# A prologue in another order: mask split and written earlier, cond turned later, presets and mask rows moved

## The reference

```python
xn = layer_norm(x, norm_w, norm_b)
q = (xn @ q_w + q_b).reshape(Bx, Tx, H, -1)
k = (xn @ k_w + k_b).reshape(Bx, Tx, H, -1)
att = jnp.einsum('bnhl,bmhl->bnmh', q, k)
att = att + (1.0 - mask) * -1000000.0
att = jax.nn.softmax(att, axis=2)
v = ((xn @ v_w + v_b) * src_mask[:, :, None]).reshape(Bx, Tx, H, -1)
y = jnp.einsum('bnmh,bmhl->bnhl', att, v).reshape(Bx, Tx, Dx)
e = jax.nn.silu(emb) @ emb_w + emb_b
scale, shift = jnp.split(e[:, None, :], 2, axis=2)
h = layer_norm(y, sb_norm_w, sb_norm_b) * (1.0 + scale) + shift
h = jax.nn.silu(h) @ out_w + out_b
return x + h
```

## Time and profile before

| | |
|---|---|
| Median of three runs | 567.2 us (567.03 to 567.59) |
| Profiled run | 564.98 us, of which the span is 563.1 us |
| TensorE busy | 542.6 us, 96% of the span |
| VectorE, ScalarE, GpSimd busy | 431.7, 371.2, 192.7 us |
| Granted TensorE clock | full in all 40 slices |
| DMA engines | 33% of the span on the SP queue, 53.74 MB in all |

### The profile page before, as it was taken

The page is one execution under the profiler, slowest core; times in us unless marked ns, Lnnn a source line. Parts: engine busy times, 40 slices in busy tenths (PEclk is TensorE's granted clock), DMA queues, the critical chain, the costliest instruction groups (busy, mean ns, idle before and its releaser), DMA issues.

```text
span 563.1 us, 10292 instructions
## 1 busy us (share of the span) xinstructions
PE 542.6 (96%) x2845; PEld 226.2 (40%) x2845; DVE 431.7 (77%) x906; ACT 371.2 (66%) x674; POOL 192.7 (34%) x238
## 2 busy tenths in 40 slices
PE   7798999999999999999999999999999999998986
PEld 3452343334443444434443444434443344423334
DVE  7399767987879877897869878897869878788422
ACT  2306866678656886677756786687756786676741
POOL 6433211445225421346205522336215432314003
PEclk9999999999999999999999999999999999999999
DMA  5650342424124333342225243242334223241021
GB/s 140 201 162 11 87 114 86 124 85 123 57 64 139 87 115 103 95 132 79 73 86 141 85 113 104 71 137 79 80 97 132 84 85 90 67 143 34 1 76 37
DMA packets 43433, 53.74 MB, mean 95 GB/s; under 512 B 11000, under 2 KB 36728, under 8 KB 43408
## 3 DMA queue, kind: packets, MB, share of 16 engines
q1 hardware_dynamic: 41360, 53.17, 32.9%
q10 hardware_dynamic: 2048, 0.27, 0.3%
HBM read 36.35 MB, written 16.80 MB: 94 GB/s over the span
## 4 chain that ended last, share of the span: by engine, by line
PE 64%; issue 12%; DMA 7%; DVE 5%; SPq 4%; POOL 3%; ACT 2%; ACTq 1%; POOLq 0%; DVEq 0%
PE pv_ps L414 16%; PE mx_ps L381 15%; PE st_ps L398 14%; PE job_ps L436 6%; DMA q_rows<-qk_dram 5%; PE job_ps L470 4%; PE job_ps L443 3%; SPq L977 2%; DVE negmax L659 2%; POOL qk_parts L855 2%; SPq L980 1%; PE job_ps L458 1%; ACT probs L515 1%; PE job_ps L449 1%; PE job_ps L453 1%
## 5 line engine op out<-in xcount | busy, mean ns | idle before, releaser
L659 DVE TENSOR_REDUCE negmax<-mx_ps 128x1 f32<-128x512 f32 x512 | 328.3, 679 | 74.5 <-PE mx_ps L381 71.3
L515 ACT ACTIVATE probs<-st_ps 128x512 f32<-128x512 f32 x512 | 278.3, 598 | 97.2 <-PE st_ps L398 96.5
L381 PE MATMUL mx_ps<-k_rows,q_rows 99*128 99x512 bf16 x512 | 195.6, 382 | 6.3 <-DMA q_rows<-qk_dram 5.6
L398 PE MATMUL st_ps<-q_rows,k_rows 101*128 101x512 bf16 x512 | 193.7, 381 | 3.3 <-DMA q_rows<-max_parts 1.2
L414 PE MATMUL pv_ps<-probs,v_rows 128*32 128x512 f32 x1024 | 136.4, 605 | 0.5 <-ACT probs L515 0.5
L381 PEld LDWEIGHTS mx_ps<-k_rows,q_rows 99*128 99x128 bf16 x512 | 50.3, 98 | 126.7 <-DVE negmax L659 85.8
L846 POOL TENSOR_TENSOR qk_rest<-qk_full,qk_parts 128x512 f32<-128x512 f32 x32 | 37.0, 1157 | 162.7 <-ACT qk_parts L525 162.6
L398 PEld LDWEIGHTS st_ps<-q_rows,k_rows 101*128 101x128 bf16 x512 | 49.8, 98 | 63.0 <-ACT probs L515 23.5
L855 POOL TENSOR_TENSOR qk_parts<-qk_rest,qk_parts 128x512 bf16<-128x512 f32 x32 | 37.1, 1158 | 68.7 <-DVE qk_parts L736 68.7
L436 PE MATMUL job_ps<-x_norm_t,w_qk 128*128 128x512 f32 x128 | 60.2, 591 | 0.0
L536 ACT ACTIVATE qk_full<-job_ps,qkb_col 128x512 f32<-128x512 f32 x32 | 22.0, 687 | 36.2 <-PE job_ps L436 36.2
(11 more groups left out here) (75 smaller groups left out, 387.8 us busy)
## 6 DMA issues: line engine op xcount, KB each, us to landing
qk_dram<-qk_parts SPq DMA_DIRECT2D x96, 128.0 KB
k_rows<-qk_dram SPq DMA_DIRECT2D x32, 192.0 KB
q_rows<-qk_dram SPq DMA_DIRECT2D x32, 192.0 KB
x_in<-in_x SPq DMA_DIRECT2D x16, 256.0 KB, 3.4
k_rows<-qk_dram SPq DMA_DIRECT2D x32, 128.0 KB
q_rows<-qk_dram SPq DMA_DIRECT2D x32, 128.0 KB
x_res<-in_x SPq DMA_DIRECT2D x8, 512.0 KB, 4.6
out<-out_sb SPq DMA_DIRECT2D x16, 256.0 KB, 2.2
```

Source lines behind the costliest of these rows:

```text
L381: pe.matmul(mx_ps[bank_of(u, MX_BANKS)][:, :], q_rows[0:ROWS_MASK, g, h, c * P:(c + 1) * P], k_rows[0:ROWS_MASK, g, h, :], start=True, sto ...
L398: pe.matmul(st_ps[bank_of(u, ST_BANKS)][:, :], k_rows[0:ROWS_ALL, g, h, c * P:(c + 1) * P], q_rows[0:ROWS_ALL, g, h, :], start=True, stop= ...
L515: act.activation(probs[:, t % P_SLOTS, h, :], st_ps[bank_of(u, ST_BANKS)][:, :], ACT.Exp).then_inc(exp_done, 1)
L659: dve.tensor_reduce(negmax[:, g % 2, h * CH + c:h * CH + c + 1], mx_ps[bank_of(GH * step + h, MX_BANKS)][:, :], AXIS_X, ALU.max, negate=Tr ...
```

## The change

- `mask_rows` runs ahead of `silu_of_cond` on VectorE (the counts of `setup_chain` follow).
- The mask parts are written to `mask_dram` from ScalarE's queue, at t = 4 of the prologue (MASK_STEP), instead of from SyncE's. SyncE no longer waits for that before the first save; it waits for `mask_saved` ahead of the first mask-row DMA.
- In `spread`, for all 32 groups, the mask-row DMA stands behind `save(2)` instead of behind `save(0)`.
- cond is turned at t = 5, behind projection 0, with its four warm matmuls (TURN_STEP and the key in WARM_FIRST).
- Both halves of `k_rows` are preset in one memset ahead of the statistics.
- GpSimd presets `v_rows` behind part 2 of group 0.

```diff
-TURN_STEP = 4
+TURN_STEP = 5
+MASK_STEP = 4
 EMBEDDING_STEP = 11
-WARM_FIRST = {4: 4, 7: 6, 9: 2}
+WARM_FIRST = {5: 4, 7: 6, 9: 2}
...
                         read_job(n, at_b, 0)
+                    if t == MASK_STEP and isinstance(b, int) and b == -1:
+                        act.wait_ge(maskp_ready, 1)
+                        act.dma_start(mask_dram[:, :, :], mask_parts[:, :, :]).then_inc(mask_saved, 16)
...
-            dve.memset(k_rows[ROWS_PROD:P, 0:NG // 2, :, :].bitcast(F32), TWO_ONES)
+            dve.memset(k_rows[ROWS_PROD:P, :, :, :].bitcast(F32), TWO_ONES).then_inc(k_preset, 1)
...
-
-                dve.memset(k_rows[ROWS_PROD:P, NG // 2:NG, :, :].bitcast(F32), TWO_ONES).then_inc(k_preset, 1)
...
                     if t == 1 and isinstance(b, int) and b == -1:
+                        mask_rows()
                         silu_of_cond()
-                        mask_rows()
...
-                if isinstance(b, int) and b == -1:
-                    presets()
-
                 take_rest(b, 3, 0)
                 take_part2(b, 3, 0)
...
                 take_rest(b, 0, 1)
                 take_part2(b, 0, 1)
+                if isinstance(b, int) and b == -1:
+                    presets()
...
-            sp.wait_ge(maskp_ready, 1)
-            sp.dma_start(mask_dram[:, :, :], mask_parts[:, :, :]).then_inc(mask_saved, 16)
-            sp.wait_ge(mask_saved, 16)
             sp.wait_ge(q_preset, 1)
             sp.wait_ge(k_preset, 1)
...
                 save(0, part0_ready)
+                save(1, part1_ready)
+                save(2, part2_ready)
+                if isinstance(b, int) and b == -1 and i == 0:
+                    sp.wait_ge(mask_saved, 16)
                 sp.dma_start(k_rows[ROWS_PROD:ROWS_MASK, i, :, :],
                              mask_dram[bass.ds(d, 1)].rearrange("a s t -> (a s) t").unsqueeze(1).broadcast_to(
                                  (PARTS, GH, T))).then_inc(rows_filled[i], 16)
-                save(1, part1_ready)
-                save(2, part2_ready)
                 fill(0)
```

More of the change, by code:

```diff
@@ L609, in mask_rows @@
                 dve.tensor_scalar(mask_bias[:, :], mask_in[:, :], -1.0, MASKED, ALU.add, ALU.mult).then_inc(setup_chain, 1)
+                dve.wait_ge(setup_chain, 1)
+                dve.tensor_copy(mask_parts[:, 0, :], mask_bias[:, :]).then_inc(setup_chain, 1)
                 dve.wait_ge(setup_chain, 2)
-                dve.tensor_copy(mask_parts[:, 0, :], mask_bias[:, :]).then_inc(setup_chain, 1)
+                dve.tensor_tensor(mask_rest[:, 0, :], mask_bias[:, :], mask_parts[:, 0, :], ALU.subtract).then_inc(setup_chain, 1)
                 dve.wait_ge(setup_chain, 3)
-                dve.tensor_tensor(mask_rest[:, 0, :], mask_bias[:, :], mask_parts[:, 0, :], ALU.subtract).then_inc(setup_chain, 1)
+                dve.tensor_copy(mask_parts[:, 1, :], mask_rest[:, 0, :]).then_inc(setup_chain, 1)
                 dve.wait_ge(setup_chain, 4)
-                dve.tensor_copy(mask_parts[:, 1, :], mask_rest[:, 0, :]).then_inc(setup_chain, 1)
+                dve.tensor_tensor(mask_rest[:, 1, :], mask_rest[:, 0, :], mask_parts[:, 1, :], ALU.subtract).then_inc(setup_chain, 1)
                 dve.wait_ge(setup_chain, 5)
-                dve.tensor_tensor(mask_rest[:, 1, :], mask_rest[:, 0, :], mask_parts[:, 1, :], ALU.subtract).then_inc(setup_chain, 1)
-                dve.wait_ge(setup_chain, 6)
                 dve.tensor_copy(mask_parts[:, 2, :], mask_rest[:, 1, :]).then_inc(maskp_ready, 1)
-                dve.memset(k_rows[ROWS_PROD:P, NG // 2:NG, :, :].bitcast(F32), TWO_ONES).then_inc(k_preset, 1)
             def silu_of_cond():
@@ L627, in silu_of_cond @@
                                          ).then_inc(setup_chain, 1)
-                dve.wait_ge(setup_chain, 1)
+                dve.wait_ge(setup_chain, 6)
                 dve.tensor_scalar(cond_silu[:, :], cond_tanh[:, :], 0.5, None, ALU.mult).then_inc(silu_ready, 1)
```

## The result

The changed kernel takes 573.6 us, the median of its executions, and the kernel before 567.1 us on the same chip: ratio 1.0131, interval 1.0107 to 1.0155. One execution of the changed kernel (909.18 us at a granted clock of 0.558) and one of the kernel before beside the first experiments (1889.44 us) lie far off and are left out of every median here. The changed kernel is slower, as forecast, but by 6.4 us (7.4 by the ratio) and not by 4.1, and 573.6 lies above the range of 568.8 to 572.7 us. The profiled execution took 574.46 us.

A forecast was written before the change was run, and what follows sets the result against it. TensorE, busy 96% of 563.1 us, was taken as the bound, so only its waits counted. Terms 3.1 + 0.8 + 0.2 = +4.1 us took the profiled 564.98 to 569.1; with 2.2 us carried over, 571.3 us, range 568.8 to 572.7.

The forecast's parts named there:

- the mask's way through ScalarE's queue: Prologue: the mask write, issued from ACT's queue, lands by about 16.3, hidden by 3 us before SyncE asks for it.
- the prologue: Up to the first fills: part 2 and the queue bound them next, so the first rows come 0.2 us later.
- the steady term: Behind the prologue: mask rows behind save(2) delay all six fills by 0.51 us; TensorE's waits grow by 3.1 + 0.8 us.
- projection 0 starts with x_norm_t: Prologue: with cond turned behind it, projection 0 starts with x_norm_t, at 12.93 plus 0.1, 0.25 us later than before.
- the 0.1 us for the restart: Prologue: 0.1 us added to projection 0's start because TensorE restarts from idle.
- The term of the memset: Prologue: one 3.51 us memset of k_rows ends at 5.19, moving statistics, x_norm and x transposes by 0.87 us.
- these six grow by the whole delay: Six TensorE waits for fills, five in group 2 and the last in group 3, each grow 0.51 us: 3.1 us.
- the two near misses: Batches whose mx matmul (368.40 and 496.27) started right behind the projection: next to no slack, 0.4 us each, 0.8 us.
- half hidden: Rival: the two near misses keep their slack and the six waits take half, 1.5 + 0.2, 568.9 us; chance 0.09.
- the other groups have over 1 us of slack: Steady part: remaining groups, such as group 3, have over 1 us of slack, so the delay adds nothing there.
- more groups begin to wait: Rival: group 3 in each batch, slack about 1.2 us, gives seven more waits of 0.2 us: 572.7 us; chance 0.09.
- the rival had it: Rival: the delayed issue is hidden in the fills' transfers, so only the prologue counts: 567.4 us; chance 0.09.

The follow-up runs named there:

- the first experiments: The first four follow-up versions, run for five rounds on one chip beside the kernel before, which had a median of 566.4 us there.
- e1: The kernel before with only the mask-row DMA moved behind save(2), in all 32 groups: 572.3 us, ratio 1.0119.
- e2: The changed kernel with the mask-row DMA back between save(0) and save(1), except in the first group: 567.4 us, ratio 1.0026.
- e6_rows_last: The kernel before with only the mask-row DMA moved behind fill(2), as the last of the group: 566.8 us, ratio 1.0017.
- e9_rows_twice_behind: The kernel before with the mask-row DMA behind save(2) and a second DMA of the same size into unused partitions behind it: 578.9 us, ratio 1.0218.
- e3_gaps_warm: The changed kernel with four more warm matmuls ahead of the x transposes and five between these and projection 0: 572.8 us, ratio 1.0106.
- after: The changed kernel itself, all edits of the change against the kernel before: 573.6 us, ratio 1.0131; its profiled execution took 574.46 us.
- after_again: The changed kernel measured once more without any edit, on another group's chip: 573.7 us, ratio 1.0121 to the kernel before.
- e10_last_warm: The changed kernel with five extra matmuls on constants ahead of TensorE's wait for the last group's fills: 572.8 us, ratio 1.0103.
- e5_half_presets: The changed kernel with the mask rows back and only half the k_rows preset ahead of the statistics, the other behind part 1 of group 0: 564.7 us.
- e7_fill_ahead: The kernel before with the first k_rows fill ahead of save(2), in all batches but the first: 564.5 us, ratio 0.9971.

## Why the prediction was right and wrong

**What held.** The delay of the fills (0.51 us in every group, nothing of it hidden on the queue), the start of projection 0 (12.92 against 12.93), the mask's way through ScalarE's queue, and the direction with its main cause. Taken alone, the mask rows cost 5.9 us, most of the 6.4. Two terms of the sum were too small, by about 2 us for the mask rows (3.9 forecast, 5.9 to 6.7 in e1) and about 1 us for the prologue (0.2 forecast, 1.0 to 1.5 in e2). That the waits sum to 9.2 us against 9.4 is luck, as the steady term below shows.

**The step "projection 0 starts with x_norm_t" was incomplete: it was priced by its start alone.** The sum gave 0.1 us for a restart from idle and carried over the 1.88 us of the earlier trace rows. Before, cond and four warm matmuls stood between the x transposes and projection 0, with at most 0.68 us idle; the change takes them away and leaves 1.31 and 1.26 us of idle time, and there the clock fell, for 1.75 us. This term should have been +1.76 and not +0.2 for the profiled execution; the 0.1 us for the restart is shown by no run. In the medians it is less: e2_rows_back, which has this prologue and the steady part of before, is only 1.0 to 1.5 us over the kernel before, where its profile shows 2.1. A likely reason is that the clock of the kernel before falls in its prologue too in some executions: to 0.50 from about 11 to 18 us in the profiles of e6_rows_last and e9_rows_twice_behind, which have its prologue unedited. What differs there is the pace of the seven warm matmuls ahead of the x transposes. Before, and then e6_rows_last:

```profile
6.08 3.17 PE L338 MATMUL pv_ps<-warm_in 128*128 128x512 bf16 x7
```

```profile
5.71 1.68 PE L338 MATMUL pv_ps<-warm_in 128*128 128x512 bf16 x7
...
9.63 1.09 PE L449 MATMUL job_ps<-ident,x_norm 128*128 128x128 f32 x8 [2.23 <-POOL x_norm L834]
```

The seven took 3.2 us in four of the 14 profiles and 1.7 us in nine (e3_gaps_warm has eleven of them), and after and after_again, the same kernel, differ in it. Where they are short TensorE idles longer behind them (0.30 us before, 2.23 here). Between them and projection 0 TensorE idled 2.57 to 4.47 us in the seven profiles in which projection 0 then took 3.6 us or more, and 0.32 to 2.93 us in the seven in which it took 1.9 to 2.0. With the changed prologue projection 0 was slow in all four profiles (after, after_again, e2_rows_back, e10_last_warm), with that of before in two of five. So the change seems to make such a fall frequent; it does not bring it in.

**The term of the memset was mis-sized.** 0.87 us forecast, 1.28 measured, the difference being the idle time ahead of it (0.91 against 0.48 us). It did not show at projection 0, because GpSimd's x_norm took 0.26 us less and the x transposes 0.26 us less. The Trainium skill (SBUF — State Buffer, "SBUF: two separate sides") says that GpSimd and a VectorE instruction on both ports exclude each other; this trace agrees in two places: x_norm took 1.77 us beside the step with two inputs and 1.51 us beside a tensor_scalar, and cond_silu took 2.34 us beside GpSimd's memset of v_rows and 0.41 us once that memset had moved. But the mask steps did not start late by it: the first ran at 9.76 us, while GpSimd's x_norm lasted until 10.51.

**The steady term, "these six grow by the whole delay", had the right cause and the wrong parts.** For the stretch from group 2 to the last group 3.4 us were forecast and 4.25 (e1_rows_behind), 4.48 (after_again) and 5.24 us (after) measured. First, the six waits did not each grow by 0.51 us: in after they grew by 0.95 us in all and not by 3.1, the two near misses by 2.1 and not by 0.8, and group 3 brought 0.6 us of new waits. Only the sum, 3.6 us, is near the 3.9. The six grew less because the last fill landed sooner. Before, for the wait at 304.57 (last fill issued, SyncE's timeline):

```profile
300.65 0.54 SPq L980 DMA_DIRECT2D q_rows<-qk_dram  x1
```

After, for the wait at 308.61:

```profile
304.99 0.54 SPq L978 DMA_DIRECT2D q_rows<-qk_dram  x1
```

That is 3.92 us from issue to matmul before and 3.62 after; for the other groups 2 that waited before it shrank by 0.1 to 0.65 us. So the "half hidden" rival was partly true. Second, "the other groups have over 1 us of slack" was wrong for group 3. The prediction read the slack from the DMA engines being idle from 125 us on the earlier trace rows. But the matmul is not released when the engines fall idle. Before, group 3 of another batch, SyncE and then TensorE:

```profile
251.16 0.54 SPq L980 DMA_DIRECT2D q_rows<-qk_dram  x1
```

```profile
254.69 0.39 PE L381 MATMUL mx_ps<-k_rows,q_rows 99*128 99x512 bf16 x1
```

The matmul comes 3.53 us behind the last fill's issue. After, where group 3 did wait (258.49), it came 3.40 us behind the issue at 255.09. So the slack was 0.13 us there, by that landing, and for 126.24 with its last fill at 122.53 some 0.3 us. A delay of 0.51 us uses that up, and group 3 waits 0.2 to 0.3 us in two to five batches: the rival "more groups begin to wait", from the wrong slack. Third, chance: in after one fill's issue took 1.30 us (its neighbours 0.6), and the wait at 503.70 became 1.33 us. The waits within this stretch account for 4.0 of its 5.24 us. Of the rest, 0.9 us is TensorE's busy time there (394.99 before, 395.87 after; 395.63 in e1_rows_behind), and what makes it longer is open.

**What the sum left out: the last wait gets long enough for the clock to fall.** It grew from 1.51 to 1.79 us and the end of the kernel by 1.60 us. Of the 14 profiled executions, the seven whose last wait was 1.61 us or less kept the clock at that place; of the seven from 1.77 to 2.42 us five lost it. e10_last_warm takes most of that back.

**The base.** The sum was made for a profiled execution whose clock was full and set on a median that is 2.2 us higher. That median already contains falls: over 68 executions of the kernel before, the 15 with a granted clock of 1.000 have a median of 564.4 us, the 25 with 0.994 and the 11 with 0.997 one of 566.4, and the 8 with 0.990 or 0.991 one of 568.5. So falls in after probably replace, in part, falls of before, and the medians differ by 6.4 us where the profiles differ by 9.3 us.

**Weighing the rule.** The Trainium skill (DMA: Bandwidth & Descriptors, "Issuing engines are not separate DMA queues") says that the time to initiate a DMA is usually small beside the DMA. Beside one DMA it is so here: 0.46 us of issue, and 3.1 to 3.9 us from the issue of a last fill to its matmul. What does not follow is that it vanishes, as the rival had it: ahead of six fills that somebody waits for, these 0.46 us cost about 1% of the kernel.

**The best versions.** A fill ahead of save(2) or the prologue without the memset and the mask rows gives 564.5 to 564.7 us, 0.3% under the kernel before, with intervals that end at 0.9993 and 0.9995. Only for the second does the profile show where it is gained.

## What to carry to other kernels

Ahead of a burst of DMAs that somebody waits for, an issue on the same queue delays the whole burst by its full time, once for each burst; keep small, early-ready DMAs in the queue's idle time, or behind the burst. Take the slack of a consumer from issue to release, as a waiting case of the same trace shows it, never from the DMA engines falling idle. And when an edit takes filler work away from TensorE or lengthens one of its idle stretches, price the work behind it at the lower clock too. A wait that grows by less than the delay, next to new waits elsewhere, can give the forecast sum by luck: compare wait by wait.

## What the runs showed of the hardware

- After idle stretches of 1.3 to 3.6 us TensorE's granted clock fell to 0.50 (1.2 GHz) for 3.4 or 6.8 us; projection 0 took 3.6 to 3.75 us there instead of 1.9, and the end of the kernel was 1.5 to 1.6 us longer. It is not certain: behind the wait at the first st matmul it fell in four profiles (1.29 to 1.34 us idle) and not in six others (1.21 to 1.35 us).
- What stood ahead of the last idle stretch seems to count too: projection 0 behind 1.26 us of idle time took 3.63 to 3.75 us in after, after_again and e10_last_warm, where TensorE had also idled 1.31 to 3.21 us ahead of the x transposes, and 1.96 us in e5_half_presets, where it had not. But e7_fill_ahead idled 2.00 and 0.93 us there and kept its clock. Once (e3_gaps_warm) the clock stayed low for some 13 us behind idle stretches of only 1.09 and 0.72 us.
- The idle time ahead of the same kind of memset on VectorE was 0.48 us for 32x2048 and 0.91 us for 32x4096, in every profile; the profile gives no releaser for it.
- A second DMA of the same form right behind the first took 0.27 us of issue (median of 32), the first 0.43 us (e9_rows_twice_behind).
